# First decoder layer: the mask of the cross query scores moves from a matmul to VectorE's maximum pass

## The reference, cut to what matters

```python
# x, c: (16, 128, 256); mask: (1, 1, 256, 256), integers
q = einsum('oi,bit->bot', wq, x) + bq      # then split into 16 heads, rotary on 4 of 8 channels
k = einsum('oi,bit->bot', wk, c) + bk
v = einsum('oi,bit->bot', wv, c) + bv
scores = einsum('bhqc,bhkc->bhqk', q, k) / sqrt(8)
scores = where(attn_mask == 0, -10000.0, scores)
p = softmax(scores, axis=-1)               # (16, 16, 256, 256)
out = einsum('bhqk,bhkc->bhqc', p, v)      # then wo, bo, residual, layer norm
```

## Time and profile before

| | |
|---|---|
| median of 3 runs | 1685.72 us (1685.56 to 1687.22) |
| span of the profiled execution | 1684.2 us |
| difference of the two | 1.5 us |
| PE busy over the span | 1400.9 us, 83% |
| DVE busy over the span | 982.0 us, 58% |
| ACT busy over the span | 609.2 us, 36% |
| first cross maximum starts / last starts | 107.6 / 583.6 us |
| cross maxima of the first layer | 256, 692 ns each |

### The profile page before, as it was taken

One profiled execution on the slowest core, in us unless ns is written; L12 is line 12 of the kernel. 1 busy time (PEld: TensorE's weight loads), 2 busy tenths in 40 slices (PEclk: granted clock), 3 DMA queues, 4 the chain that ended last, 5 costly groups with the idle time before them and its releaser, 6 DMA issues. The chain is left out here.

```text
span 1684.2 us, 29387 instructions
## 1 busy us (share of the span) xinstructions
PE 1400.9 (83%) x9221; PEld 874.6 (52%) x9331; DVE 982.0 (58%) x2623; ACT 609.2 (36%) x1389; POOL 419.8 (25%) x588
## 2 busy tenths in 40 slices
PE   2478999999999954899999946588888875999997
PEld 1245565665665522466566524455555543566654
DVE  5467788787777624222222224577788651676775
ACT  0123444544544421223222223255566542232321
POOL 2242342342341101011111023455555310000000
PEclk9679999999999976999999976799999996999999
DMA  3233443333432106611111123745454311100000
GB/s 91 59 66 60 70 72 52 72 70 55 72 67 37 24 27 226 225 32 38 32 32 33 28 56 109 159 105 114 107 116 111 85 34 50 38 1 13 13 1 26
DMA packets 165337, 112.77 MB, mean 67 GB/s; under 512 B 32690, under 2 KB 155826, under 8 KB 165056
## 3 DMA queue, kind: packets, MB, share of 16 engines
q1 hardware_dynamic: 150272, 99.04, 26.1%
q0 software_dynamic: 3408, 9.31, 2.3%
q10 hardware_dynamic: 11504, 2.53, 0.8%
HBM read 46.48 MB, written 12.45 MB: 35 GB/s over the span
## 5 line engine op out<-in xcount | busy, mean ns | idle before, releaser
L892 ACT ACTIVATE first_probs<-pair 128x512 f32<-128x512 f32 x320 | 189.0, 598 | 231.0 <-PE pair L408 217.4
L449 DVE TENSOR_REDUCE first_negmax_x<-bank 128x2 f32<-128x512 f32 x256 | 177.1, 692 | 59.7 <-PE bank L393 39.8
L393 PE MATMUL bank<-kept_stack_cross 96*128 96x256 bf16 x768 | 151.9, 280 | 11.8 <-DMA kept_stack_cross<-second_parts_x_q 7.5
L1885 ACT ACTIVATE second_probs<-pair 128x512 f32<-128x512 f32 x192 | 113.7, 598 | 130.8 <-PE pair L408 111.6
L408 PE MATMUL pair<-kept_stack_cross 98*128 98x256 bf16 x768 | 148.1, 275 | 3.0 <-ACT first_probs L892 1.0
L1439 PE MATMUL pair<-kept_w,experts_hidden_t 128*128 x312 | 140.5, 593 | 0.0
L449 DVE TENSOR_REDUCE second_negmax_x<-bank 128x2 f32<-128x512 f32 x128 | 88.6, 692 | 59.6 <-PE bank L393 50.5
L393 PEld LDWEIGHTS bank<-kept_stack_cross 96*128 96x128 bf16 x768 | 74.4, 102 | 73.0 <-issue 21.6
L1480 ACT ACTIVATE experts_hidden_t<-bank,kept_b 128x128 f32<-128x128 f32 x156 | 44.6, 368 | 186.4 <-PE bank L1414 186.4
L1394 POOL DMA_INDIRECT experts_expert_rows<-x_mid,kept_row_of x39 | 37.2, 953 | 275.6 <-PE bank L1406 249.1
L386 PE MATMUL bank<-kept_mask_q,kept_ident 128*128 128x512 bf16 x221 | 86.4, 391 | 20.4 <-DVE first_negmax_x L449 11.8
(11 more groups left out here) (430 smaller groups left out, 2947.2 us busy)
## 6 DMA issues: line engine op xcount, KB each, us to landing
kept_stack_self<-first_parts_a SPq DMA_DIRECT2D x128, 64.0 KB
kept_w<-in_L_ffn_W SPq DMA_DIRECT2D x16, 512.0 KB, 9.1
kept_w<-in_L_ffn_W SPq DMA_DIRECT2D x8, 1024.0 KB, 9.5
kept_stack_self<-second_parts_a SPq DMA_DIRECT2D x128, 64.0 KB
kept_stack_cross<-first_parts_x_k SPq DMA_DIRECT2D x96, 64.0 KB
kept_stack_cross<-first_parts_x_q SPq DMA_DIRECT2D x96, 64.0 KB
kept_stack_cross<-second_parts_x_k SPq DMA_DIRECT2D x96, 64.0 KB
kept_stack_cross<-second_parts_x_q SPq DMA_DIRECT2D x96, 64.0 KB
```

The lines of the kernel that those rows point to most:

```text
L393: mm = pe.matmul(out, q, k, start=mask is None, stop=True, skip_group_check=True)
L449: return dve.tensor_reduce(negmax[:, 2 * n:2 * n + 2], bank[:, :].rearrange("p (m t) -> p m t", t=D), AX.X, ALU.max, negate=True)
L892: act.activation(probs[i % RING][:, :], key_bank[i % 2][:, :], ACT.Exp, scale=att.scale).then_inc(probs_made, 1)
L1885: act.activation(probs[i % RING][:, :], key_bank[i % 2][:, :], ACT.Exp, scale=att.scale).then_inc(probs_made, 1)
```

## The change

The identity-by-mask matmul of the cross query scores goes, and the first score matmul of a bank now starts it (`start=mask is None`). VectorE adds the mask, and takes the maximum in the same pass: `tensor_tensor_reduce` computes (scores + mask) * -1 into a bf16 scratch tile `masked` and the minimum of it into one column of `negmax_x`. One pass takes half a bank (256 columns), so there are two for each bank. The semaphore `reduced` is raised by the second. Nothing else changes: the self attention's masks, the key round's mask matmul (L401) and the second layer stay.

```diff
+        masked = [sb(f"masked_{a}", [P, D], BF16) for a in range(2)]
...
-            mask_q, mask_t = (t[n][:, :, :].rearrange("p a k -> p (a k)") for n in ("mask_q", "mask_t"))
+            mask_t = t["mask_t"][:, :, :].rearrange("p a k -> p (a k)")
...
-                query_scores(pe, CROSS0, score_bank[i % 2], t["stack_cross0"][b % 3], n, ident16[:, :], mask_q).then_inc(scored, 1)
+                query_scores(pe, CROSS0, score_bank[i % 2], t["stack_cross0"][b % 3], n, ident16[:, :], None).then_inc(scored, 1)
...
             def cross_maximum(b, n):
                 i = query_lane.index("cross", b, n)
                 dve.wait_ge(scored, i + 1)
-                reduce_maxima(dve, CROSS0, negmax_x[:, :], score_bank[i % 2], n).then_inc(reduced, 1)
+                for a in range(2):
+                    ins = dve.tensor_tensor_reduce(masked[a][:, :], score_bank[i % 2][:, a * D:(a + 1) * D], t["mask_q"][:, a, :], -1.0, 3.0e38,
+                                                   ALU.add, ALU.min, negmax_x[:, 2 * n + a:2 * n + a + 1])
+                ins.then_inc(reduced, 1)
```

## The result

The changed kernel takes 1695.1 us in the median of 20 runs (1689.3 to 1706.7), the kernel before 1685.9 us in 20 runs beside it. The ratio is **1.0044, with a 95% interval of 1.0030 to 1.0059: slower by 0.44%**, some 7 us (the two medians alone stand at 1.0055, inside that interval). I had forecast 1724 us, 38 us more; the direction held, the size was five times too large. The profiled execution of after has a span of 1693.5 us.

A forecast was written before the change was run, and what follows sets the result against it. TensorE bounds the kernel now, VectorE after: 34.9 us a batch against 31.3, +43 us over 12.4 steady batches, ramp 0, tail -5, +38 in all: 1724 us. Range 1698 to 1757, wide range 1684 to 1765.

The forecast's parts named there:

- VectorE becomes the bound: First layer's cross attention: VectorE's need rises to 33.9 us a batch, above today's 31.3 and TensorE's 26.3.
- the 28.0 that I had for before: VectorE's need in us a batch in the kernel before, with no wait at all: 31.3 - 3.3.
- my allowance for waits: VectorE's remaining waits in the steady part after the change: 1.0 us a batch, of 3.3.
- the length of the four: Two passes and two column writes replacing a bank's reduction on VectorE: 1.06 us against 0.69, 5.9 us a batch more.
- the low bound of 0.88: Two passes and two column writes of a bank, in us, with 425 ns passes and every neighbour overlapped.
- The rule that nothing overlaps: The skill's drain rule: next operation waits for an empty pipeline; a bank's four instructions take 1.22 us, a batch 36.5.
- rival A: Cross banks: no slower, the mask matmul was the price after all; 1683 or 1678 us; chance 0.20.
- A's condition, d < 0.17: VectorE's added time per bank must stay under 0.17 us with 1.0 us of waits: four instructions in 0.86 us.
- the forecast's own: Condition of the main forecast, slower by a VectorE-bound kernel: a bank's four instructions between 0.92 and 1.22 us; chance 0.62.
- TensorE as the bound of before: Steady part, 150 to 500 us: TensorE busy 29.8 of 31.3 us a batch, full 95% of the time.
- the saving of 0.22 us a bank: Mask matmul's cost to TensorE in a cross bank: 3.5 us a batch, 56 us over 256 banks.
- The ramp and the tail: Ramp, 100 to 150 us: 0, waits absorb 10 us; tail: TensorE's saving less the longer last maximum, -5 us.

The follow-up runs named there:

- the hold: The changed kernel with GpSimd's split of the next batch's self attention held back until VectorE has made x1 of the batch in flight: 1.0009 of before.
- the four memsets: The kernel before with four 128 x 128 memsets on VectorE ahead of the tensor_scalar that makes x1: 1.0032 of before.
- TensorE's half: The kernel before without the mask matmul of the cross query scores, old reduction kept, mask left out of the row maximum: 1.0001 of before.
- the reciprocal was moved: Kernel before without the mask matmul, old reduction kept, with the reciprocal of the sums and the DMA behind it one slot later (93, not 92): 0.9936 of before.
- VectorE's half: The changed kernel with the mask matmul left in place beside the fused passes, so the mask is added twice: 1.0061 of before.
- the memset: Apparently the kernel before with one 128 x 128 memset on VectorE ahead of the tensor_scalar that makes x1: 1.0017 of before.

## Why the prediction was right and wrong

**VectorE becomes the bound: right.** Its waits fell to a third and TensorE's for it rose 2.6 times. The arithmetic that led there was of the right form too. From the window of after, 350 passes are 175 banks or 10.94 batches, 32.0 us each: VectorE is busy 293.14 / 10.94 = 26.8, has gaps of (350 - 293.14 - 12.4) / 10.94 = 4.1, and waits 1.1. Its need is 30.9 us a batch against the 28.0 that I had for before, and my allowance for waits, 1.0, was right. The count of maxima in a window is coarse, though. By the starts of L456, which stands behind the last bank of a batch, 13 batches take 406.9 us in before (128.9 to 535.7, the fourteenth) and 411.9 in after (131.3 to 543.2): 31.3 and 31.7 us each, so the steady part lost 0.4 us a batch, some 5 us, and not the 0.7 that the window's 32.0 says.

**The step that failed is the length of the four.** I took 1.06 us for them, 0.37 more than the reduction. They measured 0.77, 0.08 more, under the low bound of 0.88. The pass was 0.422 and not 0.475, the column write 0.083 and not 0.134, and the overlap was larger: the next instruction starts with the column write. The 128 x 1 rows that I took as nearest to it read inputs; it has none. To this comes what I had at zero: the drained gap in front of a slot's first pass is 0.13 us in the mean (300.21 to 300.35 is one), and in front of a reduction 0.09, another 0.04 or 0.05 a bank. Together 0.13 and not 0.37, 2.1 us a batch and not 5.9. The rule that nothing overlaps, by which I had 1.22 us, was further off still.

**A term was missing: x1's collision, 0.9 us a batch.** With 2.1 in place of 5.9 my sum would have been 28.0 + 2.1 + 1.0 = 31.1, and 12.4 x -0.2 - 5 = -7.5 us, rival A with its price: A's condition, d < 0.17, was met at 0.13, and the forecast's own, four between 0.92 and 1.22 us, was not. That the direction held is luck, since by the sum the right length gives a faster kernel. The sum lacks the 0.9: 28.0 + 2.1 + 0.9 + 1.1 = 32.1, and the window has 32.0. The row was there to be seen: 302.52 to 302.92 for x1 beside a GpSimd operation from 302.76. I had not looked at what a delay of a tenth or two would run into. Taking the 0.9 away does not bring -7.5, though. With the hold 13 batches take 407.3 us, 31.3 each and not 31.1, since half of it goes to longer waits and to L486 and L488, and the ramp and the tail fall short of my terms too. The hold and the four memsets switch the long x1 off and on; the hold was worth 6 us by the ratio.

**TensorE as the bound of before: right, but not as the only one.** From the saving of 0.22 us a bank, 56 us, TensorE's half alone brought nothing, and 11 us once the reciprocal was moved. My two-engine picture lacked the third loop through the DMA of the sums. It is why rival A's condition was too kind: under a lighter TensorE the wait for the sums rises to 2.1 us a batch, and does not shrink to 0.6 as I had it. In after it did shrink, to 3.9 / 10.94 = 0.4, since there VectorE itself was late.

**The ramp and the tail.** I had 0 and -5. The first column of two parts (L456) is made at 128.9 us in before and 131.3 in after, and the last at 584.4 and 589.9; the two last batches take 46.6 us and not 48.7. So the ramp loses and the tail gains only some 2 us. TensorE's clock in the ramp, 100 to 150 us, fell from 0.81 to 0.69, which I had not looked for. It goes with the mask matmul: the kernels that keep it stand at 0.80 to 0.86 there, those without it at 0.66 to 0.76. The halves of the change say what the ramp's loss is made of. From the first maximum to the first L456 it is 21.2 us in before and 23.7 in after, 23.2 in VectorE's half at a clock of 0.80 and 21.8 in TensorE's half at 0.76. So most of the 2.5 us comes with VectorE's half, its passes and the long x1, and not with the clock. The two ends of the stretch differ by 5.7 us; the rest of the 9 between the two spans is within what the later stages vary.

**Open:** why TensorE's half makes the transfer of the sums slower, and why VectorE's half costs as much as it does when x1 no longer collides, 1.0057 or 9 us for 16 x 0.13 = 2.1 us a batch on an engine that had 3.3 us of waits. The waits say that the two engines lose to each other within the batch, but no run took that apart.

## What to carry to other kernels

Two engines that read 95% and 79% busy may both be full: take from the second its gaps that can't be filled, and look in its queue for waits on a transfer, since a saving on the first can stop there. Before a change that shifts one engine by tenths of a microsecond, list what stands within that distance on the engine that shares its ports. And when a change gives less than its arithmetic, look first at the rows that the diff does not touch: one of them read three times its old duration here, and a wait put on another engine took most of the loss away.

## What the runs showed of the hardware that was not expected

- The fused add-and-minimum over 128 x 256 from PSUM takes 422 ns (418 to 427 in all runs), no longer than a plain two-input operation of that size (425). The read of its accumulator takes 83 ns and hides under the next instruction.
- A 128 x 256 tensor_scalar from SBUF read 277 ns behind the memset and 405 behind a reduction, though it is the same instruction, and so too in the last two batches, where no GpSimd operation stands beside it.
- In after the drained gap in front of a fused pass is 0.13 us in the mean (0.11 to 0.14), whatever instruction ended the slot before; behind an accumulator read with another instruction next it is 0.09, as in front of a reduction.
- A tensor_scalar that starts 0.02 us behind a GpSimd operation of 1.16 us reads 1.29 us; one that starts 0.06 us ahead of it reads 1.37; one that starts 0.24 us ahead reads 0.40, and GpSimd's operation then 1.18.
